# Attention projections as fp16 halves, and one ScalarE square per expert matrix, in a fused attention and expert kernel

## What is computed

```python
h = _layernorm(x, axis=-1) * (1 + ca) + sa
x = x + ga * _L0_attn_ref(h, ...)      # q, k = relu(h Wq' + bq), relu(h Wk' + bk); v = h Wv' + bv
                                       # s = gamma*s + k v'; z = gamma*z + k; y = q s / (q z + eps)
h = _layernorm(x, axis=-1) * (1 + cb) + sb
x = x + gb * _L0_ffn_ref(h, ...)       # expert = argmax(h Wr' + br); W2[e] relu(W1[e] h + b1[e]) + b2[e]
```

## Time and profile before

| | us |
|---|---|
| median of 3 runs (468.91 to 470.88) | 469.12 |
| the profiled execution | 469.77 |
| its span in the profile | 467.5 |
| TensorE busy | 439.2 (94%) |
| VectorE busy | 385.9 (83%) |
| ScalarE busy | 305.1 (65%) |
| GpSimd busy | 260.2 (56%) |

### The profile page before, as it was taken

The page is one execution under the profiler, slowest core; times in us unless marked ns, Lnnn a source line. Parts: engine busy times, 40 slices in busy tenths (PEclk is TensorE's granted clock), DMA queues, the critical chain, the costliest instruction groups (busy, mean ns, idle before and its releaser), DMA issues.

```text
span 467.5 us, 13656 instructions
## 1 busy us (share of the span) xinstructions
PE 439.2 (94%) x4296; PEld 392.0 (84%) x4296; DVE 385.9 (83%) x1012; ACT 305.1 (65%) x804; POOL 260.2 (56%) x429
## 2 busy tenths in 40 slices
PE   7999999999999999995767999999999999999992
PEld 4898889999889988893436999989999999999991
DVE  2548999999999999999985887787887777888862
ACT  1335666666666666664606877878777888778870
POOL 2112577777667766756346465656656556664332
PEclk9999999999999999997779999999999999999997
DMA  8725344444444444411015243443333443442110
GB/s 281 254 81 175 119 159 158 158 158 153 152 147 153 156 157 147 136 47 68 25 32 141 59 104 76 110 100 88 87 85 90 87 116 78 97 58 57 45 29 2
DMA packets 43572, 51.71 MB, mean 111 GB/s; under 512 B 24811, under 2 KB 37356, under 8 KB 41328
## 3 DMA queue, kind: packets, MB, share of 16 engines
q1 hardware_dynamic: 37552, 36.67, 27.1%
q0 software_dynamic: 4992, 12.60, 9.8%
q10 hardware_dynamic: 960, 1.57, 1.0%
HBM read 35.22 MB, written 13.50 MB: 104 GB/s over the span
## 4 chain that ended last, share of the span: by engine, by line
PE 76%; DVE 13%; issue 3%; DMA 3%; DVEq 2%; ACT 1%; POOL 1%; ACTq 0%; POOLq 0%
PE ps_o L1434 17%; PE ps_qk L1351 11%; PE ps_qk L1420 9%; PE ps_va L1420 9%; PE ps_va L1361 6%; PE ps_o L1310 5%; PE ps_kv L1317 5%; PE ps_va L1338 3%; PE ps_o L1306 3%; DVE w L1123 2%; DMA w<-in_wmod 2%; DVE arena L1109 2%; PE ps_k L1189 2%; DVEq L1127 1%; PE ps_x L1231 1%
## 5 line engine op out<-in xcount | busy, mean ns | idle before, releaser
L1434 PE MATMUL ps_o<-w,arena 128*128 x936 | 108.7, 273 | 0.6 <-DVE arena L1109 0.4
L1434 PEld LDWEIGHTS ps_o<-w,arena 128*128 128x128 f16 x936 | 89.8, 98 | 10.9 <-issue 1.2
L1123 DVE COPY w<-w 128x2048 f16 x78 | 59.2, 760 | 34.5 <-PE ps_va L1420 23.9
L660 ACT ACTIVATE arena<-ps_qk,arena 128x128 f32<-128x128 f32 x156 | 44.6, 368 | 41.9 <-PE ps_qk L1420 39.1
L1351 PE MATMUL ps_qk<-arena,wqk_b 128*128 128x128 f32 x512 | 62.4, 275 | 0.0
L1420 PE MATMUL ps_qk<-arena,w 128*128 128x128 f16 x936 | 58.7, 219 | 3.6 <-DVE w L1123 1.9
L544 POOL DMA_INDIRECT out_rows<-arena,slot_token x39 | 42.1, 1081 | 34.5 <-POOL arena L540 30.6
L1351 PEld LDWEIGHTS ps_qk<-arena,wqk_b 128*128 128x128 f32 x512 | 59.7, 192 | 0.0
L1420 PEld LDWEIGHTS ps_qk<-arena,w 128*128 128x128 f16 x936 | 55.2, 98 | 5.3 <-issue 2.4
L1420 PE MATMUL ps_va<-arena,w 128*128 128x128 f16 x936 | 58.6, 219 | 0.2 <-DVE w L1123 0.2
L1109 DVE TENSOR_TENSOR arena<-arena 128x512 f16<-128x512 f32 x78 | 53.3, 683 | 4.7 <-ACT arena L668 3.7
(11 more groups left out here) (192 smaller groups left out, 834.2 us busy)
## 6 DMA issues: line engine op xcount, KB each, us to landing
w<-in_w_raw SPq DMA_DIRECT2D x16, 1024.0 KB, 5.1
token_rows<-arena SPq DMA_DIRECT2D x64, 128.0 KB, 1.9
arena<-in_x SPq DMA_DIRECT2D x32, 128.0 KB, 2.1
b_sb<-in_b2b SPq DMA_DIRECT2D x1, 1024.0 KB, 5.3
w<-in_wmod ACTq DMA_DIRECT2D x1, 768.0 KB, 8.7
w<-in_wqkv SPq DMA_DIRECT2D x1, 768.0 KB, 8.1
arena<-token_rows,slot_token POOLq DMA_INDIRECT x39, 3.6
out_rows<-arena,slot_token POOLq DMA_INDIRECT x39
```

The source lines that it names most:

```text
L660: last = act.activation(hid[:, f, :], bank[("qk", "va")[h]][:, (f % 4) * P:(f % 4 + 1) * P], ACT.Relu, bias=consts_now[:, r, f:f + 1], sca ...
L1123: dve.tensor_copy(now[:, :, i * F // 2:(i + 1) * F // 2], of[:, :, i * F // 2:(i + 1) * F // 2]).then_inc(s_w1, 1)
L1434: last = pe.matmul(bank[f"o{n % 2}"][:, 0:D], hid_parts[:, r % 2, b, f, :], w[:, bass.ds(m, 1), a, f * D:(f + 1) * D].rearrange("p a d -> ...
```

## The change

The projections of q, k and V no longer multiply in fp32. The weights (with the modulation and a common power-of-two scale) and the transposed h are each kept as a high and a low fp16 half, and three products replace one: high x high, high x low, low x high. The high half of h is the old copy L616, now to fp16; the low half is a new VectorE instruction (`h_lo`) behind it. The scales need bounds over the weights, which are new steps in the head (`qk_bound`, `qk_scales`, `v_scales`), and the parts of the head are put in a new order. The results are scaled back in `decay`, the biases, `den_eps` and L994.

The four maxima of an expert matrix are replaced by one ScalarE instruction that squares 2048 elements and adds them up (`square_matrix`; two of 1024 for the last three matrices), placed in the even slot before the evictions of q and k. The sum product L1335 moves to the odd slot of the same iteration, and the scale is made there. `hi_piece` and `lo_piece` take their quarters in other slots.

The second norm (L592) moves on ScalarE from before the evictions of q and k to behind them. The token bound and scale move from slots (1, 0) and (1, 1) into (1, 0). The diff, cut:

```diff
+        def squared(m):
+            return m + 1 + (HALVES - 1) * max(m + 1 - LANDS, 0)
...
+            def square_matrix(k):
+
+                if (m := matrix_at(k, MAX)) is None:
+                    return
+                act.wait_ge(s_wraw, 16 * (m + 1))
+                if m == 0:
+                    act.wait_ge(s_piece, 1)
+                if m < LANDS:
+                    act.activation(w[:, m, 0, :], raw_w[:, landing(m), :], ACT.Square,
+                                   accum_out=w_piece[:, m, 0:1]).then_inc(s_wboth, 1)
+                    return
+                for i in range(HALVES):
+                    need(act, s_wboth, squared(m - 1) + i)
+                    half = raw_w[:, landing(m), i * (MW // HALVES):(i + 1) * (MW // HALVES)]
+                    act.activation(squares, half.rearrange("p (b c) -> p b c", b=B), ACT.Square,
+                                   accum_out=w_piece[:, m, i:i + 1]).then_inc(s_wboth, 1)
...
-                if (m := matrix_at(k, HI + 1 - u)) is not None:
+                if (m := matrix_at(k, HI)) is not None:
                     if isinstance(m, int) and (m == NM - 1) != last:
                         return
-                    i = 2 * (1 - u) + j
+                    i = 2 * u + j
...
-                if it := att_item(k, u, NORM2):
-                    n, g, r = it
-                    act.wait_ge(s_rs2, n // B + 1)
-                    need(act, s_h2, n - 1)
-                    q = g % 2
-                    act.activation(xn2[:, r, :], x1_sb[:, r, q, 0:D], ACT.Identity, bias=rs2[:, q, r, 2:3],
-                                   scale=rs2[:, q, r, 1:2]).then_inc(s_xn2, 1)
+                if u == 0 and k > 0:
+                    square_matrix(k)
                 if it := att_item(k, u, PROJ):
...
+                if it := att_item(k, u, NORM2):
...
                 hi_piece(k, u, 0)
                 if it := att_item(k, u, XPOSE):
 
                     n, g, r = it
                     act.wait_ge(s_xt, n + 1)
                     need(act, s_vp, n - 1)
-                    act.activation(h_t[:, r], bank["x"][:, 0:D].rearrange("p (k t) -> p k t", k=DK),
-                                   ACT.Copy).then_inc(s_ht, 1)
+                    act.activation(h_t[:, r, 0], bank["x"][:, 0:D].rearrange("p (k t) -> p k t", k=DK),
+                                   ACT.Copy, scale=X_ONE).then_inc(s_hhs, 1)
...
                 if k == -1:
                     act.wait_ge(s_wqkv, 32)
-                    act.wait_ge(s_modt_ready, 1)
+                    act.wait_ge(s_ss, 1)
                     for h in range(DK):
-                        last = act.activation(wqk_b[:, u, :, h, :], wqkv_sb[:, 0:2, h, :], ACT.Copy,
-                                              scale=scale_at[:, h, u:u + 1])
-                    last.then_inc(s_wqk, 1)
+                        last = act.activation(wqk_b[:, u, 0, :, h, :], wqkv_sb[:, 0:2, h, :], ACT.Copy,
+                                              scale=scale_qk[:, h, u:u + 1])
+                    last.then_inc(s_whq, 1)
+                if (k, u) == (-1, 1):
+                    act.wait_ge(s_sv, 1)
+                    for b in range(B):
+                        act.activation(wv_b[:, b, 0], wv_f[:, b], ACT.Copy, scale=v_scale).then_inc(s_whv, 1)
                 hi_piece(k, u, 1)
+                if (k, u) == (0, 0):
+                    square_matrix(k)
 
...
+            def qk_bound():
+                dve.wait_ge(s_wqkv, 32)
+                dve.tensor_reduce(qk_most[:, 0:1], wqkv_sb[:, 0:2].rearrange("p m h d -> p (m h d)"), AX_X, ALU.max,
+                                  apply_absolute_value=True)
+                dve.wait_ge(s_modt_ready, 1)
+                step(dve.tensor_reduce(qk_most[:, 1:2], scale_at, AX_XY, ALU.max, apply_absolute_value=True))
+                dve.tensor_tensor(qk_most[:, 0:1], qk_most[:, 0:1], qk_most[:, 1:2], ALU.mult).then_inc(s_qkm, 1)
...
+            def power_of_two(largest, scale, whole, back):
+
+                step(dve.tensor_scalar(head_bits.bitcast(I32), largest.bitcast(I32), EXPONENT, None, ALU.bitwise_and))
+                step(dve.tensor_scalar(scale.bitcast(I32), head_bits.bitcast(I32), -1.0, float((TOP + 254) * EXP_ONE),
+                                       ALU.mult, ALU.add))
+                dve.tensor_scalar(back.bitcast(I32), head_bits.bitcast(I32), float(-(TOP + 10) * EXP_ONE), None, ALU.add)
+                step(dve.tensor_scalar(whole, scale, X_ONE, None, ALU.mult))
+
+            def qk_scales():
+                power_of_two(qk_sum, qk_scale, qk_all, qk_back)
+                dve.tensor_scalar(scale_qk[:], scale_at, qk_scale, None, ALU.mult).then_inc(s_ss, 1)
+                dve.tensor_scalar(decay[:], decay[:], qk_back, qk_back, ALU.mult, ALU.mult).then_inc(s_decayed, 1)
+
...
+            def qk_lo(b):
+                dve.wait_ge(s_whq, b + 1)
+                for h in range(DK):
+                    last = dve.scalar_tensor_tensor(wqk_b[:, b, 1, :, h, :], wqkv_sb[:, 0:2, h, :],
+                                                    scale_qk[:, h, b:b + 1], wqk_b[:, b, 0, :, h, :], ALU.mult,
+                                                    ALU.subtract)
+                last.then_inc(s_wqk, 1)
+
+            def v_scales():
+                dve.wait_ge(s_wvs, 1)
+                step(dve.tensor_scalar(v_sum, bank["o0"][:, 0:1], 2.0 ** -20, None, ALU.max))
+                power_of_two(v_sum, v_scale, v_all, v_back)
+                dve.memset(scales[:, 15:16], 0.0).then_inc(s_sv, 1)
+                dve.tensor_scalar(den_eps, v_all, DEN_EPS, None, ALU.mult)
+                dve.wait_ge(s_init, INIT)
+                dve.tensor_copy(v_ext[:, :, DX:DZ], v_all.unsqueeze(1).to_broadcast([P, B, 1]))
+
+            def v_lo(b):
+                dve.wait_ge(s_whv, b + 1)
+                dve.scalar_tensor_tensor(wv_b[:, b, 1], wv_f[:, b], v_scale, wv_b[:, b, 0], ALU.mult,
+                                         ALU.subtract).then_inc(s_wvb, 1)
+
+            def h_lo(k, u):
+                if it := att_item(k, u, XPOSE):
+                    n, g, r = it
+                    dve.wait_ge(s_hhs, n + 1)
+                    dve.scalar_tensor_tensor(h_t[:, r, 1], bank["x"][:, 0:D].rearrange("p (k t) -> p k t", k=DK),
+                                             X_ONE, h_t[:, r, 0], ALU.mult, ALU.subtract).then_inc(s_ht, 1)
+
...
-                dve.tensor_copy(of_width[:, :, :, DX:DV], u_t[:]).then_inc(s_wvb, 1)
+                step(dve.tensor_copy(of_width[:, :, :, DX:DV], u_t[:]))
+                step(dve.tensor_reduce(v_most[:, 0:1], wv_f.rearrange("p b h c -> p (b h c)"), AX_X, ALU.max,
+                                       apply_absolute_value=True))
+                dve.memset(scales[:, 14:15], 0.0).then_inc(s_wvm, 1)
...
 
-            def max_piece(k, u, j):
-
-                if (m := matrix_at(k, MAX)) is None:
+            def lo_piece(k, u, j, last=False):
+
+                if (m := matrix_at(k, LO - u)) is None or (m == NM - 1) != last:
                     return
...
+                i = 2 * (1 - u) + j
...
                 if (k, u) == (-1, 0):
+                    qk_bound()
                     router_scale()
+                    qk_scales()
+                    router_centre()
                     v_weights(0)
-                    router_centre()
                     v_weights(1)
+                    h_lo(-1, 1)
+                    qk_lo(0)
+                    router_columns()
                     projection_biases()
+                    v_scales()
+                    v_lo(0)
+                    qk_lo(1)
+                    v_lo(1)
...
-                        dve.tensor_reduce(w_most, bank["va"][:, W_AT:W_AT + PIECES + 1], AX_X, ALU.max).then_inc(s_wmax, 1)
+                    if u == 1 and (m := matrix_at(k, MAX)) is not None:
+                        dve.tensor_reduce(w_most, bank["va"][:, W_AT:W_AT + HALVES + 1], AX_X, ALU.add).then_inc(s_wmax, 1)
                     need(dve, s_o, n - 1)
...
-                max_piece(k, u, 0)
...
-                if (k, u) == (FULL, 1):
-                    scale_matrix(NM - 1)
-                    for j in range(1, PIECES - 1):
-                        lo_piece(k, j // 2, j % 2)
+                h_lo(k, u)
                 if (k, u) == (2, 0):
                     consts16()
-                if u == 0 and k < FULL and (m := matrix_at(k, HI)) is not None:
+                if u == 1 and (m := matrix_at(k, MAX)) is not None:
                     scale_matrix(m)
                 if (k, u) == (1, 0):
+                    token_bound()
+                    token_scale()
+                if (k, u) == (1, 1):
                     gate(gate_bt, tiny_raw).then_inc(s_gbt, 1)
-                    token_bound()
-                if (k, u) == (1, 1):
-                    token_scale()
-                max_piece(k, u, 1)
 
             slots(dve, *ATT, slot)
...
-            lo_piece(FULL, 1, 1)
```

(32 more changed lines are left out.)

120 lines of the change are left out of this document (69 added, 51 removed).

## The result

The changed kernel takes 478.62 us (477.79 to 481.09), the kernel before on the same chip 469.34 (468.91 to 470.88). The ratio is 1.0211, with a 95% interval of 1.0184 to 1.0238: slower by 2.1%, where 466.8 was forecast and 475 was the upper end of the range.

The account below looks back on a forecast made before the run. TensorE was taken to bound the kernel before, at 11.89 us an iteration, and the ring after, at 11.5. Head 3.1, loop -5.6 and tail +0.2 gave -2.3: 467.5 us profiled, 466.8 against the median; range 459 to 475.

Parts of the forecast that it names:

- Prices of single operations: Attention loop: q and k 1.34 us, V 0.69, ScalarE's square 2.0, VectorE's low half of h 0.47.
- the ring: Attention loop: odd q and k (start X), evictions, norm, GpSimd, even norm, h, odd q and k; 11.5 us an iteration.
- VectorE is relieved by 1.7 us in all and is no bound: Attention loop: four maxima leave VectorE (2.7 us), low half of h comes in twice, 0.47 us each.
- Rounds: ... 3.15, so X + 8.8 with no hold: GpSimd's two rounds of inverse deviations in the loop: 3.15 us, ending 8.8 us after odd q and k start.
- the late hold: Even slot: VectorE's L880 from X + 8.4 to 9.1 holds the rounds' last small GpSimd instructions to X + 9.3 to 9.65.
- not held: Rival for the loop: small GpSimd instructions end before L880 starts; iteration 11.0 us, 460.3 us in all; chance 0.15.
- Rival (c): Loop: the hold works both ways, L880 ends later; iteration 12.1 us, 474.6 us in all; chance 0.28.
- The head: Work before the steady loop: new bounds and scales delay chunk 0 to 22.1 us; +3.1 us by chunk 5, bounds +1.5 and +5.
- The late setup behind it is as long as before: Head, after V of chunk 0: setup length unchanged, so chunk 1 at 32.7 instead of 29.47 us, +3.2.
- The floors: Slot (1, 1), second iteration: token bound and scale precede the product waiting for the floors; TensorE waits about 2.7 us.
- The pace of 5.2 a chunk gives it back: Second iteration: the wait of 2.7 us is recovered; chunk 4 at +3.0 us, chunk 5 at +3.1.
- The tail: From chunk 31 to the expert loop: +0.2 us, bounds -1.6 and +1.

Follow-up runs that it names:

- second: Changed kernel with the second norm ahead of the evictions again in the odd slots alone; 1.0019 of the kernel before, 468.58 us.
- fourth: Changed kernel with a fourth fp16 product (low x low) in q, k and V; 1.0386 of the kernel before, 485.87 us.
- tenth experiment: Changed kernel with GpSimd's gating product ahead of the two operations of the second norm in every slot; 0.9985 of the kernel before.
- thirteenth experiment: Changed kernel with only the even slot's first low piece (L970) replaced by a maximum over 512 elements; pace 11.54 us an iteration, only the loop compared.
- first experiment: Changed kernel with eleven TensorE products of zeros more in the head's two gaps (seven and four); 1.0214 of the kernel before.
- fifth: The first experiment with ten more products of zeros ahead of the first norm-sum product's wait for the square; 1.0144 of the kernel before.
- seventh: Changed kernel with the first experiment's fillers, the first two norm-sum products behind V, and the odd norm ahead of the evictions; 0.9898, 465.29 us.
- fifteenth: The seventh without fillers, with VectorE's token bound and scale moved to the start of slot (1, 0); 0.9840 of the kernel before, 462.05 us.
- third: Changed kernel with the square over a quarter of each matrix (512 elements, not 2048) for the first matrices; 1.0172 of the kernel before.
- twelfth: Changed kernel with each low piece of an expert matrix (L970) replaced by a maximum over 512 elements; pace 10.95 us, only the loop compared.
- eighth: Changed kernel with the second norm ahead of the square and the evictions in both slots; 1.0502 of the kernel before, 493.09 us.

## Why the prediction was wrong

**Prices of single operations: right.** q and k cost 1.34 (99.47 to V at 100.81), V 0.69, the square 1.90 to the next instruction (told 2.0), the low half 0.53 to TensorE's start (told 0.53).

**That the ring binds: right for every second iteration.** It was named with all its links, and the second, fourth and tenth experiments show it from three sides. In the iterations between, TensorE does not wait for h but for the scores, behind a VectorE that started late and has no gap. The step "VectorE is relieved by 1.7 us in all and is no bound" failed: V waits 0.91 and 0.52 us there, and 11.14 us is the steady iteration where the ring is open and VectorE full (tenth experiment).

**The ring's length: wrong by one hold.** From X = 99.47:

| | told | measured |
|---|---|---|
| evictions | X + 1.54 | 1.54 |
| L493 starts | 3.21 | 3.24 |
| L503 done, L461 starts | 5.67 | 5.78 |
| first L461 costs | 0.28 | 0.72 |
| L470 ends | 9.3 to 9.65 | 9.88 |
| next odd q and k | 11.5 to 11.8 | 11.95 |

The step that failed is "Rounds: ... 3.15, so X + 8.8 with no hold". The even slot's first L970, at X + 5.25 beside the first L461, was not in the list of holds, though the prediction placed the two others. It costs 0.44 us in every second iteration: five times between chunks 7 and 27 the first L461 has 0.64 to 0.66 us, and the odd chunk that follows is each time one that waits for h; otherwise it has 0.19 or 0.20. That L970 is itself 0.38 longer, and the work behind it on VectorE, up to the L970 of the late hold, comes at X + 8.90 and not 8.4. The thirteenth experiment shows the ring without that one hold: 11.50 in the iteration in which the late hold remains (11.5 to 11.8 forecast), and where none of the rounds is held h allows a start 10.98 behind the last (11.0 forecast for "not held"; low half at 106.88, X = 96.43). Its mean of 11.54 is near the forecast by chance, being a mean of 11.1 and 11.9.

Rival (c) had the right size (12.1), with another mechanism: the second L970 of the even slot is 0.74 us here and not over 0.8. The longer one is the first, 1.12, and it starts while GpSimd is in L503. So both do wait for each other, at the place that the prediction had left out. Of the sum: -5.6 was told, -0.1 came. How much of the 5.5 us is the hold's and how much VectorE's queue's stays open, since each late h makes VectorE start late in the next iteration and no experiment parts the two.

**The head: wrong by 6.5 us.** Chunk 0 came at 21.58 (told 22.1), V of chunk 0 at 24.32 (told 25.0): VectorE's order was read rightly. The step that failed is "The late setup behind it is as long as before". The change puts the sum of the first matrix into slot (0, 1) and its square at the end of ScalarE's slot (0, 0). The prediction has no term for this; it put the wait at nothing without a reason, though it counted the like wait in slot (1, 1). TensorE can't have that sum before 32 us (first experiment). The other part is the clock. Chunk 1 was told at 32.7 and came at 37.49. With the clock held up past the wait it came at 34.11 (fifth), and with the sum moved away too and the clock at 1.00 at 32.10 and 32.20 (seventh, fifteenth). So 3.4 us are the clock's and 2.0 the wait's. Moving the sum away brings chunk 1 to between 32.1 and 34.3 in five kernels. In the profile of the changed kernel the wait can't be seen, because TensorE came to it late, at half clock.

**The floors: the wait right, its end wrong.** 2.7 us were told and 2.71 came. "The pace of 5.2 a chunk gives it back" did not hold: chunk 4 was told at +3.0 and stands at +9.6, chunk 5 likewise. A loop that runs at 11.9 as before gives nothing back. That the wait isn't the sum's alone was missed too: VectorE's 2.9 us of token bound delay the scores, and V waits for these when the sum no longer does.

**The tail: right.** +0.2 was told, with bounds of -1.6 and +1; from chunk 31 to the expert loop it is -0.2.

The sum was 3.1 - 5.6 + 0.2; it came out as 9.6 - 0.1 - 0.2. Two terms are off by 6.5 and 5.5 us, and both in the direction of slower, so the range of 459 to 475 did not hold them. Its width came from single bounds (head to +5, ring to 12.1), and a head and a ring both beyond their middle were never added. The head's 9.6 lies outside even its own bound.

What stays open is when the clock falls. The kernels agree up to 24 us but for the fillers, and with the same two gaps the clock from 24 to 28 us was 0.50 in three profiles (the changed kernel, the third, the tenth), 0.77 and 0.81 in two (the thirteenth, the twelfth) and 1.00 in four (the second, fourth, eighth and fifteenth).

## What to carry to other kernels

When products get cheaper, write down the ring through every other engine with all instructions beside which a two-input VectorE operation can stand, slot by slot, and not only at the places where the trace of before shows a hold. Ask of every late operand what the engine that waited for it does next: here VectorE's late start cost the next iteration as much, and two iterations had to be read to see it. An operation moved behind another on one engine has to be checked in both halves of an unrolled loop: here its odd half cost the loop its gain, and putting one GpSimd operation ahead of two others gave 0.7 us an iteration back. In a head, ask of every semaphore that moves to an earlier slot when its producer runs there; a slow clock can hide the wait from the profile.

## What the hardware showed

- GpSimd and VectorE wait for each other only in some pairs. Beside L970, whose two inputs lie in SBUF, a GpSimd instruction of 0.20 us took 0.64 or 0.71. Beside a maximum over the same 512 elements it took 0.20. The Trainium skill (GPSIMD Engine Reference, Specifications) has contention with VectorE instructions that have two SBUF inputs; the twelfth kernel agrees. The hold goes both ways: L970 has 0.74 us alone and 1.12 where L503 was under way. L1091, with two SBUF inputs as well, has 0.19 or 0.20 alone (changed kernel) and up to 0.76 beside GpSimd in the tenth kernel, where such stretched records fill the queue that sets the pace.
- The same two gaps in TensorE's work, 1.9 and 1.2 us long, were followed by a granted clock of 0.50 from 24 us on in the profile of the changed kernel, and by 1.00 in that of the fifteenth. From V of chunk 0 to chunk 1 there are 13.17 us at 0.50, 12.35 where the clock falls only behind the wait for the square (first experiment), and 10.09 at 1.00 all the way (fifth): filling the first gaps alone moves the fall to the next wait.
- A loop with one of two holds removed does not settle at a length in between. In the thirteenth kernel it goes from 11.1 to 11.9 and back, and 11.54 is only the mean. The changed kernel alternates too, between a wait for h and waits for the scores, at nearly the same length each time.
